# Query and key projections of a Flamingo block: evacuated 128 partitions wide into staging tiles, with DMAs placing the halves

## The chip, the core and the metric

The kernel runs on one core of one Trainium2 chip. Its time is the device time of one execution, in microseconds, as the median of repeated runs. TensorE (PE), VectorE (DVE), ScalarE (ACT) and GpSimd (POOL) each run their own instruction list, and SyncE (SP) issues all the DMAs. The engines meet only at semaphores.

## What is computed

A gated cross-attention layer, then a gated mixture of experts, for 8 batches of 512 tokens with 256 channels. The context has 512 rows of 128 channels; there are 16 heads of 64.

```
h = layernorm(x)
q, k, v = h @ Wq, ctx @ Wk, ctx @ Wv            # 16 heads of 64
out = softmax(q k^T / 8) v @ Wo + bo
x = x + tanh(g_xattn) * out
h2 = layernorm(x);  top-2 of 8 experts by softmax(h2 @ gate_w^T)
x = x + tanh(g_ffn) * sum_e comb_e * (h2 @ W_e^T + b_e)
```

## The kernel before

**Precision.** Most products are made from split operands: a value is rounded to fp32r ("hi") and the rest is kept as a second fp32r tile ("lo"). A projection is then three matmuls for each pair of tiles (hi·hi, hi·lo, lo·hi). ACT makes the hi part from PSUM, then DVE subtracts it from PSUM to get the lo part.

**Batches and slots.** Every engine walks the same order: batch, head h of 16, tile t of 4 (128 queries). One (h, t) is a slot. The first batch (FIRST), six in a hardware loop of two rounds of three (LOOP) and the last (LAST) have the same slots; EPI finishes the experts of the last batch. In each slot TensorE does two things for attention: the scores of tile (h, t), transposed, as two matmuls into a bank of ST (`scores`, L1044 and L1047), and one plain score matmul into a bank of MX for a tile six slots ahead (`maximum`, L1037). DVE reduces the MX bank to a row maximum (L767), SyncE carries the 128 maxima by a DMA into one row of QB (`row`, L432), and L1047 adds them to the scores, so that exp needs no further shift. ACT takes the exp (L596) and copies it to fp16 (L621), POOL makes its lo part (L514), and `values` (L1057) multiplies by V once per head. MX and ST have two banks each.

**Jobs.** Everything else is a list of jobs written out by hand in `PLACED`, which says in which slot TensorE makes it: `q`, `k`, `v` projections, `ot` (turned outputs), `wo`, the router and the experts of the batch before. Jobs share three PSUM banks; `job_ready` counts those made by PE, `job_hi` those that ACT has taken, `job_free` those whose bank is free again. A pair of heads p has a job ("q", p) and a job ("k", p), each a bank of 128 partitions (head 2p in partitions 0 to 63, head 2p+1 in 64 to 127) by 512 tokens. Pairs 2 to 7 are made in the batch itself, pairs 0 and 1 of the next batch in heads 12 to 15. q is made at (0,2), (2,3), (4,2), (6,1), (8,1), (10,1), (12,1), (14,1), and k at (1,1), (3,0), (5,0), (7,0), (8,3), (10,3), (12,3), (14,3); a job is taken by ACT and DVE one slot later (`taken_in`).

**The tiles of the scores.** For each head, QA holds the hi part of q in both halves of the partitions, KA the hi part of k above its lo part, KB the hi part of k, and QB the lo part of q, with the row of maxima in partition 64 (and ones there in KB). So L1044 gives hi·hi + lo·hi and L1047 gives hi·lo and the shift. All four tiles have six places, that is three pairs of heads.

**Evacuation of q and k.** The two heads of a job lie in different halves of the bank, so each is moved by its own instruction of 64 partitions: ACT writes QA[0:64] or KA[0:64] twice (L552, L553), DVE writes QB[0:64] (L739) or KA[64:128] (L744) twice. One DMA of 256 KB then copies QA[0:64] to QA[64:128], or KA[0:64] to KB[0:64], for both heads (`copy`, L427). TensorE waits for these copies at the first slot of a pair (`k_dup`) and, for a pair ahead, at (h even, 2) (`q_dup`).

**SyncE's order.** In `step`, for each slot: the row of the maximum, then the copy of a q or k job whose hi part is taken in that slot. Between batches it stores `acc` (L477) and loads `kvin` (L450). At head 5 it loads the next x (L467). In FIRST it also loads Wo and the expert weights (L457).

Of the kernel before, what the change touches and what calls it, by code (L numbers as in the profile page):

```python
# [177 lines left out]
class Iteration:  # L178
# [9 lines left out]
    def pair_slot(self, name):  # L188

        ahead = PAIRS if self.kind != PRO and name in NEXT_JOBS else 0  # L190
        return self.head_slot(2 * (name[1] + ahead))

    def start(self, lists):
# [46 lines left out]
def build(nc, x, kv_t, g_xattn, g_ffn, wq, wk, wv, wo, bo, gate_t, expert_t, expert_b, out):  # L240
# [5 lines left out]
    with ctx:  # L246
# [96 lines left out]
        job_ready, job_hi, job_free = sem("job_ready"), sem("job_hi"), sem("job_free")  # L343
        q_dup = [sem("q_dup0"), sem("q_dup1")]
        k_dup = [sem("k_dup0"), sem("k_dup1")]
        max_ready, max_free = sem("max_ready"), sem("max_free")
# [22 lines left out]

        def dup_count(b, p):  # L370
            return 16 * (b * (PAIRS // 2) + (p // 2 + 1))

# [33 lines left out]
        def _(sp):  # L406
# [11 lines left out]

            def copy(it, name):

                kind, p = name
                s = it.pair_slot(name)
                heads = slice(s, s + 2)
                dst, src, copied = ((QA[HEAD:P, heads, :], QA[0:HEAD, heads, :], q_dup) if kind == "q" else
                                    (KB[0:HEAD, heads, :], KA[0:HEAD, heads, :], k_dup))
                sp.wait_ge(job_hi, it.done(HI, name))
                sp.dma_start(dst.bitcast(F32), src.bitcast(F32)).then_inc(copied[p % 2], 16)  # L427

            def row(it, h, t):

                sp.wait_ge(max_free, tile_count(it.b, h, t) + 2)
                sp.dma_start(QB[HEAD:HEAD + 1, it.head_slot(h), t * P:(t + 1) * P].bitcast(F32),  # L432
                             nmax[:, h % 2, t:t + 1].bitcast(F32), allow_slow_non_contiguous=True)\
                  .then_inc(row_in[h % 2], 16)

            pro = Iteration(PRO, 0, 0)
            for name in [name for name in JOBS[PRO] if name[0] in "qk"]:
                if name == ("q", 1):
                    for t in range(TT):
                        row(pro, 0, t)  # L440
                copy(pro, name)
            for t in range(TT // 2):
# [10 lines left out]
            def step(it, h):  # L453
# [84 lines left out]
        def _(act):  # L538
# [6 lines left out]
            def take_hi(it, name):  # L545
# [3 lines left out]
                kind = name[0]  # L549
                if kind in ("q", "k"):  # L550
                    dst, s = (QA if kind == "q" else KA), it.pair_slot(name)
# [90 lines left out]
        def _(dve):  # L642
# [44 lines left out]
            def take(it, name):  # L687
# [47 lines left out]
                dve.wait_ge(job_hi, it.done(HI, name))  # L735
                if kind == "q":
                    s = it.pair_slot(name)
# [189 lines left out]
        def _(pe):  # L927
# [112 lines left out]
            def scores(it, h, t):  # L1040

                b, s = it.b, it.head_slot(h)
                pe.wait_ge(st_free, tile_count(b, h, t))
                pe.matmul(st_bank(h, t)[:, :], KA[:, s, tile(t)], QA[:, s, :], start=True, stop=False)  # L1044
                if t == 0:
                    pe.wait_ge(row_in[h % 2], row_count(b, h))
                pe.matmul(st_bank(h, t)[:, :], KB[0:HEAD + 1, s, tile(t)], QB[0:HEAD + 1, s, :],  # L1047
                          start=False, stop=True).then_inc(st_ready, 1)
# [16 lines left out]
            for name in JOBS[PRO]:  # L1065
# [6 lines left out]
                if name == ("q", 1):  # L1072
                    pe.wait_ge(job_free, pro.done(JOBS, ("k", 0)) + BANKS)
                    pe.wait_ge(q_dup[0], dup_count(0, 0))
                    for t in range(TT):
# [6 lines left out]
            def slot(it, h, t):  # L1082
                b, kind = it.b, it.kind
                p, ahead = h // 2, (h + 2) // 2 % PAIRS
                if h % 2 == 0 and t == 0:
                    pe.wait_ge(k_dup[p % 2], dup_count(b, p))
                for part in PE_ORDER[h % 2][t].split():
                    if part == "scores":
                        scores(it, h, t)
                    elif part == "maximum":  # L1090
                        if maximum_at(kind, h, t):
                            if h % 2 == 0 and t == TT // 2:
                                pe.wait_ge(job_free, (it.done_before if ahead == 1 else it.done)(JOBS, ("k", ahead))
                                           + BANKS)
                                pe.wait_ge(q_dup[ahead % 2], dup_count(b if ahead else b + 1, ahead))
                            maximum(it, *maximum_at(kind, h, t))
# [41 lines left out]
```

## Time and profile before

| | |
|---|---|
| runs | 1210.83, 1213.07, 1218.82 us |
| median | 1213.07 us |
| profiled execution | 1210.17 us, of which the span of instructions is 1208.5 us |
| granted TensorE clock | 0.989 |
| busy: PE, DVE, ACT, POOL | 94%, 81%, 70%, 54% |
| mean DMA queue load (q1) | 20.3% of 16 engines |

The span runs from the first to the last instruction. A matmul is pipelined and its end is modelled, so a PE that is 94% busy may still lose time between matmuls; what it waited for stands in the chain of waits and in the idle times ahead of a group. The first batch lies at about 9 to 154 us, the six looped ones from 154 to 1018 us, the last up to 1145 us, and the rest is the epilogue.

### The profile page before, as it was taken

The numbers are of one execution on the slowest core, as the hardware profiler recorded it, in microseconds if no ns is written. First come the engines' busy times: TensorE is split into PE (matmuls) and PEld (weight loads), VectorE is DVE, ScalarE is ACT, GpSimd is POOL, SyncE is SP. The second block draws the span as 40 slices with busy tenths as digits, with TensorE's granted clock in tenths as the row PEclk, the third lists the DMA queues.
The fourth block names the chain that finished last, engine by engine and source line by source line (L and its number), as shares of the span: only waits on it lengthen the run. The fifth ranks groups of instructions, "written<-read, shape, count | busy, mean of one in ns | idle before, by whom it ended". The sixth has DMA issues, their size and how long they took to land.

```text
span 1208.5 us, 30873 instructions
## 1 busy us (share of the span) xinstructions
PE 1135.7 (94%) x10592; PEld 913.4 (76%) x10592; DVE 979.0 (81%) x1945; ACT 849.6 (70%) x1531; POOL 648.0 (54%) x579
## 2 busy tenths in 40 slices
PE   4888999999999999999899999999999999999968
PEld 3677777788778887788777887778877788778846
DVE  7788878987898778987789877898778887897646
ACT  4888888676876678676786768867687677866610
POOL 2566666455655547455564545645556455654610
PEclk8999999999999999999999999999999999999979
DMA  4333212122221122221222112211122121121000
GB/s 133 78 85 79 37 37 54 29 37 45 37 53 29 28 54 36 46 37 27 57 37 45 28 37 45 54 36 28 41 50 45 28 37 40 33 37 36 2 19 17
DMA packets 97521, 51.79 MB, mean 43 GB/s; under 512 B 77000, under 2 KB 86608, under 8 KB 97360
## 3 DMA queue, kind: packets, MB, share of 16 engines
q1 hardware_dynamic: 97360, 49.74, 20.3%
q8 instruction: 89, 1.46, 0.5%
q14 instruction: 72, 0.59, 0.2%
HBM read 11.68 MB, written 4.19 MB: 13 GB/s over the span
## 4 chain that ended last, share of the span: by engine, by line
PE 70%; DVE 15%; issue 7%; DMA 3%; ACT 3%; SPq 1%; DVEq 0%; POOL 0%; ACTq 0%
PE MB L934 30%; PE PV L1057 12%; PE MX L1037 8%; PE ST L1047 7%; PE ST L1044 7%; DVE nmax L767 3%; DVE KA L744 3%; PE MB L944 3%; DMA QB<-nmax 2%; DVE QB L739 1%; PE MB L1014 1%; DVE stats L656 1%; DVE w L879 1%; SPq L432 1%; DVE m L886 1%
## 5 line engine op out<-in xcount | busy, mean ns | idle before, releaser
L514 POOL TENSOR_TENSOR p_s<-pf,p_s 128x512 f16<-128x512 f32 x512 | 594.7, 1169 | 496.1 <-ACT p_s L621 492.5
L596 ACT ACTIVATE pf<-ST 128x512 f32<-128x512 f32 x512 | 306.2, 599 | 193.0 <-PE ST L1047 186.3
L767 DVE TENSOR_REDUCE nmax<-MX 128x1 fp32r<-128x512 f32 x512 | 347.2, 685 | 69.0 <-PE MX L1037 60.9
L621 ACT ACTIVATE p_s<-pf 128x512 f16<-128x512 f32 x512 | 318.1, 629 | 45.1 <-PE PV L1057 42.0
L1037 PE MATMUL MX<-KA,QA 128*128 128x512 f32 x512 | 216.9, 426 | 18.6 <-DVE nmax L767 15.2
L1057 PEld LDWEIGHTS PV<-v_s,p_s 128*128 128x128 f16 x6144 | 193.6, 98 | 33.6 <-issue 24.7
L1047 PE MATMUL ST<-QB,KB 65*128 65x512 f32 x512 | 204.8, 400 | 7.2 <-DMA QB<-nmax 7.0
L1057 PE MATMUL PV<-v_s,p_s 128*128 128x65 f16 x6144 | 209.0, 194 | 1.3 <-POOL p_s L514 1.3
L1044 PE MATMUL ST<-QA,KA 128*128 128x512 f32 x512 | 206.2, 403 | 3.6 <-ACT pf L596 3.1
L934 PE MATMUL MB<-ex_s,x2t_s 128*128 128x512 f32 x708 | 188.8, 402 | 3.2 <-DVE KA L744 3.2
L934 PEld LDWEIGHTS MB<-ex_s,x2t_s 128*128 128x128 f32 x708 | 128.1, 188 | 34.9 <-DVE KA L744 6.3
L1037 PEld LDWEIGHTS MX<-KA,QA 128*128 128x128 f32 x512 | 97.1, 190 | 54.3 <-DVE nmax L767 32.6
L722 DVE SCALAR_TENSOR_TENSOR acc<-MB,comb,acc 128x256 f32<-128x256 f32 x236 | 113.8, 482 | 23.6 <-PE MB L934 16.5
L1047 PEld LDWEIGHTS ST<-QB,KB 65*128 65x128 f32 x512 | 96.3, 188 | 31.8 <-DMA QB<-nmax 13.4
L1044 PEld LDWEIGHTS ST<-QA,KA 128*128 128x128 f32 x512 | 97.0, 189 | 23.0 <-issue 6.7
L934 PEld LDWEIGHTS MB<-wo_s,ot_s 128*128 128x128 f32 x768 | 100.0, 188 | 7.2 <-DVE ot_s L754 1.7
L934 PE MATMUL MB<-xt_s,wq_s 128*128 128x512 f32 x384 | 102.3, 402 | 1.7 <-issue 1.5
L934 PE MATMUL MB<-wo_s,ot_s 128*128 128x256 f32 x768 | 101.5, 282 | 1.4 <-DVE ot_s L754 1.4
L739 DVE TENSOR_TENSOR QB<-MB,QA 64x512 fp32r<-64x512 f32 x128 | 87.6, 684 | 17.7 <-ACT QA L553 16.8
L744 DVE TENSOR_TENSOR KA<-MB,KA 64x512 fp32r<-64x512 f32 x128 | 88.3, 690 | 14.0 <-ACT KA L553 10.2
L934 PEld LDWEIGHTS MB<-xt_s,wq_s 128*128 128x128 f32 x384 | 73.9, 193 | 19.9 <-issue 1.8
L754 DVE TENSOR_TENSOR ot_s<-MB,ot_s 128x512 fp32r<-128x512 f32 x64 | 44.2, 690 | 46.0 <-ACT ot_s L559 45.4
(120 smaller groups left out, 1113.4 us busy)
## 6 DMA issues: line engine op xcount, KB each, us to landing
QA<-QA SPq DMA_DIRECT2D x64, 256.0 KB, 3.0
KB<-KA SPq DMA_DIRECT2D x64, 256.0 KB, 3.0
QB<-nmax SPq DMA_DIRECT2D x512, 0.5 KB, 1.9
xin<-x SPq DMA_DIRECT2D x8, 512.0 KB, 4.0
out<-acc SPq DMA_DIRECT2D x8, 512.0 KB, 3.2
kvin<-kv_t SPq DMA_DIRECT2D x8, 256.0 KB, 4.2
acc<-expert_t SPq DMA_DIRECT2D x8, 256.0 KB, 3.3
acc<-wo SPq DMA_DIRECT2D x4, 256.0 KB, 3.3
```

The source lines that it names most:

```text
L514: pool.tensor_tensor(p_s[:, h % 2, 1, t, :], pf[:, t, :], p_s[:, h % 2, 0, t, :], ALU.subtract)\
L596: act.activation(pf[:, t, :], st_bank(h, t)[:, :], ACT.Exp, bias=P_SHIFT, scale=SCALE)\
L621: act.activation(p_s[:, h % 2, 0, t, :], pf[:, t, :], ACT.Copy).then_inc(p_hi, 1)
L722: last = dve.scalar_tensor_tensor(acc[:, t, :], m[:, DIM * i:DIM * (i + 1)], comb[:, t, 2 * e + i:2 * e + i + 1], acc[:, t, :], ALU.mult, ...
L739: last = dve.tensor_tensor(QB[0:HEAD, s + i, :], m[HEAD * i:HEAD * i + HEAD, :], QA[0:HEAD, s + i, :].bitcast(F32), ALU.subtract)
L744: last = dve.tensor_tensor(KA[HEAD:P, s + i, :], m[HEAD * i:HEAD * i + HEAD, :], KA[0:HEAD, s + i, :].bitcast(F32), ALU.subtract)
L767: dve.tensor_reduce(nmax[:, h % 2, t:t + 1], MX[t % 2][:, :], AX.X, ALU.max, negate=True)\
L934: last = pe.matmul(dst, s, m, start=(k == 0), stop=(k == n - 1))
L1037: pe.matmul(MX[t % 2][:, :], QA[:, s, tile(t)], KA[:, s, :], start=True, stop=True)\
L1044: pe.matmul(st_bank(h, t)[:, :], KA[:, s, tile(t)], QA[:, s, :], start=True, stop=False)
L1047: pe.matmul(st_bank(h, t)[:, :], KB[0:HEAD + 1, s, tile(t)], QB[0:HEAD + 1, s, :], start=False, stop=True).then_inc(st_ready, 1)
L1057: last = pe.matmul(PV[:, t * (HEAD + 1):(t + 1) * (HEAD + 1)], p_s[:, h % 2, i, k, tile(t)], v_s[:, j, k, h % HEADS, :], start=(k == 0 and ...
```

## The change

In LOOP, FIRST and LAST (not in the prologue, PRO), ACT moves a q or k job with one instruction of 128 partitions into a staging tile, `q_hl[:, 0]` or `k_hl[:, 0]`, and DVE writes the rest into `[:, 1]` with one instruction. DMAs of 128 KB then place the halves, two for each placement. `copy_first`, one slot later than `copy` stood, issues four: for q both halves of QA; for k both KA[0:64] and then, after a wait for `job_free`, both KA[64:128]. `copy_second(it, h)`, at the first slot of an even head, issues four for the next pair: KB[0:64] and QB[0:64] in turn, because KB and QB now have four places (two pairs) in place of six, and the pair that held them must be through. Each pair so takes 12 DMAs of 128 KB where it took two of 256 KB. New waits: ACT, before it fills a staging tile, waits for the copies of the pair before out of it (and for DVE to have used it); DVE waits likewise before a lo part; TensorE waits at (h even, 0) for KB and QB and at (h even, 2) for QA and KA of the following pair.

```diff
@@ tiles @@
-        QB = sb("QB", [P, 2 * SLOTS, TOKENS], F32R)
+        QB = sb("QB", [P, 4, TOKENS], F32R)
-        KB = sb("KB", [P, 2 * SLOTS, TOKENS], F32R)
+        KB = sb("KB", [P, 4, TOKENS], F32R)
+        q_hl = sb("q_hl", [P, 2, TOKENS], F32R)
+        k_hl = sb("k_hl", [P, 2, TOKENS], F32R)
@@ sync @@
+            def copy_first(it, name):
+                kind, p = name
                 s = it.pair_slot(name)
                 sp.wait_ge(job_hi, it.done(HI, name))
+                for i in range(2):
+                    rows = slice(HEAD * i, HEAD * (i + 1))
+                    if kind == "q":
+                        sp.dma_start(QA[0:HEAD, s + i, :].bitcast(F32), q_hl[rows, 0, :].bitcast(F32))\
+                          .then_inc(qa_in[p % 2], 16)
+                        sp.dma_start(QA[HEAD:P, s + i, :].bitcast(F32), q_hl[rows, 0, :].bitcast(F32))\
+                          .then_inc(qa_in[p % 2], 16)
+                    else:
+                        sp.dma_start(KA[0:HEAD, s + i, :].bitcast(F32), k_hl[rows, 0, :].bitcast(F32))\
+                          .then_inc(ka_in[p % 2], 16)
+                if kind == "k":
+                    sp.wait_ge(job_free, it.done(JOBS, name) + BANKS)
+                    for i in range(2):
+                        rows = slice(HEAD * i, HEAD * (i + 1))
+                        sp.dma_start(KA[HEAD:P, s + i, :].bitcast(F32), k_hl[rows, 1, :].bitcast(F32))\
+                          .then_inc(ka_in[p % 2], 16)
+
+            def copy_second(it, h):
+                p = h // 2 + 1
+                if h == 0:
+                    sp.wait_ge(job_free, it.start(JOBS) + BANKS)
+                else:
+                    sp.wait_ge(job_free, it.done(JOBS, ("k", p % PAIRS)) + BANKS)
+                for i in range(2):
+                    rows = slice(HEAD * i, HEAD * (i + 1))
+                    sp.dma_start(KB[0:HEAD, 2 * (p % 2) + i, :].bitcast(F32), k_hl[rows, 0, :].bitcast(F32))\
+                      .then_inc(kb_in[p % 2], 16)
+                    sp.dma_start(QB[0:HEAD, 2 * (p % 2) + i, :].bitcast(F32), q_hl[rows, 1, :].bitcast(F32))\
+                      .then_inc(qb_in[p % 2], 16)
...
                     if maximum_at(it.kind, h, t):
                         row(it, *maximum_at(it.kind, h, t))
-                    for name in taken_in(it.kind, h, t):
-                        if name[0] in "qk":
-                            copy(it, name)
+                    if h % 2 == 0 and t == 0 and not (it.kind == FIRST and h == 0) and \
+                            not (it.kind == LAST and h == HEADS - 2):
+                        copy_second(it, h)
+                    if (h, t) != (0, 0):
+                        for name in taken_in(it.kind, *((h, t - 1) if t else (h - 1, TT - 1))):
+                            if name[0] in "qk":
+                                copy_first(it, name)
@@ scalar, take_hi @@
+                if kind in ("q", "k") and it.kind != PRO:
+                    p = name[1]
...
+                    before = p - 1 if p >= 2 else p - 1 + PAIRS
+                    if not early_pair(it, before):
+                        if kind == "q":
+                            act.wait_ge(qa_in[before % 2], qa_count(it, before))
+                        else:
+                            act.wait_ge(ka_in[before % 2], ka_count(it, before))
+                            act.wait_ge(kb_in[before % 2], kb_count(it, before))
+                    last = act.activation((q_hl if kind == "q" else k_hl)[:, 0, :], m[:, :], ACT.Copy)
@@ vector, take @@
+                if kind in ("q", "k") and it.kind != PRO:
...
+                    if not early_pair(it, before):
+                        if kind == "q":
+                            dve.wait_ge(qb_in[before % 2], qb_count(it, before))
+                        else:
+                            dve.wait_ge(ka_in[before % 2], ka_count(it, before))
+                    last = dve.tensor_tensor(hl[:, 1, :], m[:, :], hl[:, 0, :].bitcast(F32), ALU.subtract)
@@ tensor @@
                 if h % 2 == 0 and t == 0:
-                    pe.wait_ge(k_dup[p % 2], dup_count(b, p))
+                    pe.wait_ge(kb_in[p % 2], kb_count(it, p))
+                    if not early_pair(it, p):
+                        pe.wait_ge(qb_in[p % 2], qb_count(it, p))
...
                             if h % 2 == 0 and t == TT // 2:
...
+                                    pe.wait_ge(ka_in[following % 2], ka_count(it, following))
+                                pe.wait_ge(qa_in[following % 2], qa_count(it, following))
```

## Rows read from the trace of the kernel before

**Rows 1.** The profile page: chain of waits by engine and by line.
```profile
PE 70%; DVE 15%; issue 7%; DMA 3%; ACT 3%; SPq 1%; DVEq 0%; POOL 0%; ACTq 0%
PE MB L934 30%; PE PV L1057 12%; PE MX L1037 8%; PE ST L1047 7%; PE ST L1044 7%; DVE nmax L767 3%; DVE KA L744 3%; PE MB L944 3%; DMA QB<-nmax 2%; DVE QB L739 1%; PE MB L1014 1%; DVE stats L656 1%; DVE w L879 1%; SPq L432 1%; DVE m L886 1%
```

**Rows 2.** Table by stretch, one looped batch.
```profile
core 0: us, PE busy (x) PEld busy (x) DVE busy (x) ACT busy (x) POOL busy (x), PEclk, DMA share, GB/s
...
296.60:440.30 143.70, 139.78 (x1326) 113.16 (x1325) 119.82 (x240) 105.56 (x191) 80.08 (x71) 1.00 0.20 40
```

**Rows 3.** Chain of waits of 370 to 441 us, by line.
```profile
by line: PE MB L934 44.3%; PE PV L1057 14.5%; PE MX L1037 9.7%; PE ST L1044 9.7%; PE ST L1047 9.6%; PE MB L944 3.7%; issue 2.1%; PE MB L1014 1.8%; DVE nmax L767 1.0%; ACT ot_s L559 0.8%; DVE acc L722 0.8%; SPq L477 0.7%; SPq L432 0.7%; PE M
```

**Rows 4.** Groups by shape: busy us, mean ns, idle before and its releaser.
```profile
L739 DVE TENSOR_TENSOR QB<-MB,QA 64x512 fp32r<-64x512 f32 x128 | 87.6, 684 | 17.7 <-ACT QA L553 16.8
...
L754 DVE TENSOR_TENSOR ot_s<-MB,ot_s 128x512 fp32r<-128x512 f32 x64 | 44.2, 690 | 46.0 <-ACT ot_s L559 45.4
...
L553 ACT ACTIVATE QA<-MB 64x512 fp32r<-64x512 f32 x64 | 38.1, 596 | 0.7
...
L559 ACT ACTIVATE ot_s<-MB 128x512 fp32r<-128x512 f32 x64 | 38.1, 595 | 5.0 <-PE MB L944 5.0
```

**Rows 5.** DMA issues: size, median us to landing.
```profile
QA<-QA SPq DMA_DIRECT2D x64, 256.0 KB, 3.0
...
QB<-nmax SPq DMA_DIRECT2D x512, 0.5 KB, 1.9
```

**Rows 6.** Timeline of SyncE: a copy and the rows behind it.
```profile
480.98 0.54 SPq L427 DMA_DIRECT2D QA<-QA  x1
```

**Rows 7.** Landing of the row issued at 481.6, by its line.
```profile
L432 SPq DMA_DIRECT2D QB<-nmax x1: 533/533/533, 481.6 to 481.6; - x1
...
DMA to landing us min/median/max: 3.1/3.1/3.1
```

**Rows 8.** Chain of waits of 440 to 446.5 us: start, us, what.
```profile
441.70 0.78 SPq L432
...
442.60 3.45 DMA QB<-nmax
...
446.09 0.50 PE ST L1047
```

**Rows 9.** Timeline, third batch, heads 0 to 2: start, us, idle in brackets.
```profile
301.73 1.39 DVE L739 TENSOR_TENSOR QB<-MB,QA 64x512 fp32r<-64x512 f32 x2 [1.14 <-ACT QA L553]
...
308.17 1.39 DVE L744 TENSOR_TENSOR KA<-MB,KA 64x512 fp32r<-64x512 f32 x2 [1.06 <-ACT KA L553]
...
311.60 4.95 SPq L432 DMA_DIRECT2D QB<-nmax  x4
...
314.82 0.40 PE L1037 MATMUL MX<-KA,QA 128*128 128x512 f32 x1
```

**Rows 10.** Timeline, heads 2 to 4 of the same batch.
```profile
320.09 1.38 DVE L739 TENSOR_TENSOR QB<-MB,QA 64x512 fp32r<-64x512 f32 x2
...
324.83 1.39 DVE L744 TENSOR_TENSOR KA<-MB,KA 64x512 fp32r<-64x512 f32 x2
...
327.63 4.73 SPq L432 DMA_DIRECT2D QB<-nmax  x4
...
331.61 0.40 PE L1037 MATMUL MX<-KA,QA 128*128 128x512 f32 x1
```

**Rows 11.** Timeline, heads 6 and 7, DVE.
```profile
352.17 1.38 DVE L739 TENSOR_TENSOR QB<-MB,QA 64x512 fp32r<-64x512 f32 x2
...
359.78 1.39 DVE L744 TENSOR_TENSOR KA<-MB,KA 64x512 fp32r<-64x512 f32 x2
```

**Rows 12.** Chain of waits of 100 to 125 us, first batch.
```profile
102.86 0.69 DVE KA L744
...
105.82 1.88 DMA QB<-nmax
...
107.75 0.50 PE ST L1047
```

More of the change, by code:

```diff
@@ L191, in pair_slot, with copied @@
         return self.head_slot(2 * (name[1] + ahead))
+    def copied(self, p):
+        return 4 * self.b + p // 2
     def start(self, lists):
@@ L368, in head_count, with qa_count, ka_count, qb_count @@
             return b * HEADS + (h + 1)
-        def dup_count(b, p):
-            return 16 * (b * (PAIRS // 2) + (p // 2 + 1))
+        def qa_count(it, p):
+            return 64 * it.copied(p) + 16
+        def ka_count(it, p):
+            return 64 * it.copied(p)
+        def qb_count(it, p):
+            return 32 * it.copied(p)
+        def kb_count(it, p):
+            return 32 * it.copied(p) + 16
+        def early_pair(it, p):
+            return it.kind == FIRST and p < 2
         late = [(wo[256 * k:256 * (k + 1), :].rearrange("(c p) n -> p c n", p=P),
@@ L417, in _, with copy_early @@
             sp.dma_start(gt_f[:, :, :], gate_t.rearrange("(c p) e -> p c e", p=P)).then_inc(small_in, 16)
-            def copy(it, name):
+            def copy_early(it, name):
+                kind, p = name
+                heads = slice(2 * p, 2 * p + 2)
+                dst, src, copied = ((QA[HEAD:P, heads, :], QA[0:HEAD, heads, :], qa_in) if kind == "q" else
+                                    (KB[0:HEAD, heads, :], KA[0:HEAD, heads, :], kb_in))
+                sp.wait_ge(job_hi, it.done(HI, name))
+                sp.dma_start(dst.bitcast(F32), src.bitcast(F32)).then_inc(copied[p % 2], 16)
@@ L440, in _ @@
                         row(pro, 0, t)
-                copy(pro, name)
+                copy_early(pro, name)
             for t in range(TT // 2):
@@ L735, in take @@
                 dve.wait_ge(job_hi, it.done(HI, name))
-                if kind == "q":
+                if kind in ("q", "k") and it.kind != PRO:
+                    p = name[1]
+                    before = p - 1 if p >= 2 else p - 1 + PAIRS
+                    hl = q_hl if kind == "q" else k_hl
+                    if not early_pair(it, before):
[4 more added lines that the diff above has]
+                    last = dve.tensor_tensor(hl[:, 1, :], m[:, :], hl[:, 0, :].bitcast(F32), ALU.subtract)
+                elif kind == "q":
                     s = it.pair_slot(name)
@@ L1046, in scores @@
                     pe.wait_ge(row_in[h % 2], row_count(b, h))
-                pe.matmul(st_bank(h, t)[:, :], KB[0:HEAD + 1, s, tile(t)], QB[0:HEAD + 1, s, :],
+                pe.matmul(st_bank(h, t)[:, :], KB[0:HEAD + 1, h % 4, tile(t)], QB[0:HEAD + 1, h % 4, :],
                           start=False, stop=True).then_inc(st_ready, 1)
@@ L1073, in _ @@
                     pe.wait_ge(job_free, pro.done(JOBS, ("k", 0)) + BANKS)
-                    pe.wait_ge(q_dup[0], dup_count(0, 0))
+                    pe.wait_ge(qa_in[0], 16)
                     for t in range(TT):
@@ L1092, in slot @@
                             if h % 2 == 0 and t == TT // 2:
-                                pe.wait_ge(job_free, (it.done_before if ahead == 1 else it.done)(JOBS, ("k", ahead))
-                                           + BANKS)
-                                pe.wait_ge(q_dup[ahead % 2], dup_count(b if ahead else b + 1, ahead))
+                                following = h // 2 + 1
+                                if early_pair(it, following):
+                                    pe.wait_ge(job_free, it.start(JOBS) + BANKS)
+                                else:
+                                    pe.wait_ge(ka_in[following % 2], ka_count(it, following))
+                                pe.wait_ge(qa_in[following % 2], qa_count(it, following))
                             maximum(it, *maximum_at(kind, h, t))
```

20 lines of the change are left out of this document (11 added, 9 removed).

## Prediction

> **What bounds the kernel now.** I read the chain of waits first, because an average share of busy time hides which wait ends last. It is 70% TensorE and 15% DVE; the second halves of the k evacuations (L744) are 3% of it and those of q (L739) 1% [rows 1]. So TensorE sets the pace in most places, and DVE in some. The table by stretch says the same of one looped batch: of 143.7 us TensorE is busy 139.8, DVE 119.8 and ACT 105.6 [rows 2]. Then I read the chain batch by batch. From head 8 on (370 to 441 us) it is TensorE nearly throughout, and no evacuation of q or k is among its entries [rows 3]: whatever the change saves or delays there by less than the slack of DVE and ACT is worth nothing. The stretches where an evacuation does end the wait are four: the row of maxima that TensorE awaits at the start of head 1 [rows 8], k of pair 2 in head 1 [rows 9], q and k of pair 3 [rows 10], q and k of pair 5 with the routing around them [rows 11]. The rest of the argument is about these four, seven times over, and about the first batch.
>
> **What the wide instructions save.** One DVE instruction of 64 partitions takes 684 ns, one of 128 partitions 690 ns; for ACT it is 596 and 595 ns [rows 4]. The width costs nothing, so each q or k job loses a whole instruction: 0.7 us of DVE and 0.6 us of ACT. For 124 such jobs outside the prologue that is 85 us of DVE and 74 us of ACT, but it counts only in the stretches above. k of pair 2: DVE stood idle 1.06 us until ACT had made the second half [rows 9], so both savings lie in line, 1.3 us. Pair 3: two of DVE's instructions go, in a stretch where DVE works without a break, 1.4 us. Pair 5: again 1.4 us. Together 4.1 us a batch, if nothing else becomes late.
>
> **What the DMAs cost.** A copy of 256 KB lands 3.0 us after its issue, a row of 0.5 KB 1.9 us [rows 5]; a copy of 128 KB lies between, and halfway, 2.45 us, is my value, with both ends kept. Issuing one costs SyncE 0.54 us, and the next begins 0.64 after it [rows 6, 7]: four take 2.4 us. Half of the 1.1 us of transfer is about 0.55 us, a little under the pace of issue, so within a burst nothing should pile up much. The Trainium skill (DMA: Bandwidth & Descriptors, "Rules for kernel authors") says that two transfers to disjoint partition halves aren't worth splitting, because both use the same 16 engines and serialize. That speaks against the two halves of each placement. The same page's fit (its cost of one DMA, 2.0 us and the bytes at 436 GB/s) gives an estimate of 2.3 us for 128 KB, by which each sum below would come out 0.15 us lower. The trace shows the sharing: a row issued right behind a copy landed after 3.1 us and not 1.9 [rows 7].
>
> **Where k now arrives by DMA.** Before, DVE wrote the lo part of k into KA in place. Now SyncE issues it after the row of slot (h, t) two slots behind the job. Call M the end of DVE's maximum there. The row takes 0.5 us, then come four issues, the last beginning at M + 2.3 and landing at M + 4.8 (4.2 to 5.3 with the ends above). TensorE wants it at its `maximum` of slot (h even, 2), and `scores`, `values` or jobs are queued behind that.
> - Pair 2: SyncE's row issue at 311.60 marks M, and TensorE's maximum is at 314.82, 3.2 us later [rows 9]. With M 1.3 us earlier, KA is there at old M + 3.5. So the stage gains nothing and loses 0.3 us (gain of 0.3 to loss of 0.8).
> - Pair 3: 327.63 and 331.61 [rows 10], 4.0 us. M is 1.4 us earlier, KA at old M + 3.4: a gain of 0.6 us instead of 1.4 (0.1 to 1.2).
> - Pair 5 has the same four slots, but with two expert jobs in them, so TensorE comes later; pairs 6, 7, 0 and 1 have a slot more, 2.2 us (143.7 / 64). I take these as in time. The gain of 1.4 us stays.
>
> **The rows behind `copy_second`.** In slot (h even, 0) four issues now stand between the row of that slot and the next. A slot takes 2.2 us on average, so SyncE is mostly free again in time, and the row of head h + 1, tile 3, is wanted only three slots later. The exception is h = 0. SyncE comes there late from storing `acc` and loading `kvin`; its first row is issued at 441.70 to 442.48, the decisive one at 442.60, it lands 3.45 us later and TensorE starts at once [rows 8]. Four issues in between move the second to 445.0. The backlog of the store will be through by then, so I take 2.6 us to landing (between the 1.9 of a free queue and 3.45 as now), 447.6 in place of 446.05: a loss of 1.6 us (0.9 to 2.4). Here the DMA is on the path that sets the end in every batch from the second on. DVE waits at the same time: the lo part of q of pair 2 may begin only when QB of pair 1 has been copied out, about 442.5 + 2.4 + 2.4 = 447.3. Its like in the batch before began at 301.73, after 1.14 us of idle time [rows 9], one batch of 143.7 us earlier than 445.4. This 1.9 us lies beside TensorE's stall and I cost it at nothing; without that cover it would be another 1 us.
>
> **The same wait elsewhere.** For the other q jobs the lo part comes two slots after `copy_second`, some 4 us, against 0.5 + 1.8 + 2.45 = 4.75 after M. DVE will stand idle up to 0.7 us and has one instruction of 0.7 us less to do: even. In heads 8 to 15 DVE's slack covers it.
>
> **Sum of a looped batch.** +0.3 - 0.6 - 1.4 + 1.6 = -0.1 us; seven batches about -1 us. With all ends good it is -0.3 - 1.2 - 1.4 + 0.9 = -2.0 a batch, -14 in all; with all bad, and half of pair 5's gain lost, +0.8 - 0.1 - 0.7 + 2.4 = +2.4, +17 in all.
>
> **First batch.** It has no expert jobs, so slots are shorter, and TensorE is often released by a row: an evacuation of k ends at 103.55, the row takes 1.88 us from 105.82, and the matmul begins at 107.75 [rows 12]. My estimates, from that one row and the prices above: six heads in which a burst stands before such a row, at 1.0 us each (0.6 of issue and 0.7 of landing, less some slack), 6 us; with KA of pairs 2 and 3, where less time is left than in a looped batch, 4 us; and with about 12 evacuations on the chain that lose an instruction, 0.7 us each, 8 us. Net +2 us (-6 to +10). In the last batch head 13 is released by its row in the same way: +1 us. The prologue keeps its own evacuations.
>
> **Total.** -1 + 2 + 1 = +2 us on the profiled 1210.2 us. The median of the runs is 2.9 us above that execution, so 1215 us. Within 1% is what a measurement of this kernel can't tell from no change: 1201 to 1225.
>
> **Rivals.**
> - *Bursts that pile up (slower).* If the copies of a burst hold up one another, so that the last lands 3.5 us or more after its issue, every burst becomes a wait: KA of pairs 2 and 3 comes 1 us later than reckoned, the row of head 1 lands after 3.45 us, and the rows of heads 2 and 5, just behind a burst of q or of `copy_second`, come late too. At 1 us for each of these that is some 4 us a batch above my sum, 28, and in the first batch 8: 1250 us, 1240 if only part of it shows. It decides from a landing of M + 5.5. For it: rows behind one copy already land 1.2 us late [rows 7], and traffic per pair goes from 0.5 to 1.5 MB. Against it: 0.55 us of transfer at an issue every 0.6. 0.18.
> - *DVE waits for QB (slower).* If the lo part of q waits over 1 us in each pair, and DVE's queue with its maxima behind it, the second halves of the batches lose too: 5 pairs by 0.5 us by 7, 17 us: 1232 us. Against it: DVE is 83% busy there and waits for TensorE between. 0.09.
> - *The savings go through (faster).* If a copy of 128 KB lands in little over 1.9 us and SyncE's delay at head 0 is hidden by the backlog that now holds up the row, the good ends apply: -14 - 6 - 0 gives 1193 us. For it: the chain names these evacuations [rows 1]. 0.13. That the wide instructions save nothing is excluded by rows 4.
> - *My forecast*, 1203 to 1225: 0.60.
>
> **Range and chances.** 1200 to 1236 leaves out the far part of the first and third rival, 2 in 10. Faster by over 1%: 0.13. Slower by over 1%: the two slower rivals less their near edge, 0.25. Within: 0.62.
>
> **What the profile after should show.** Evacuations of q and k as 62 instructions each of 128x512 on ACT and DVE, beside the prologue's of 64; DVE busy about 85 us less, ACT about 73 less. TensorE waiting for KA by DMA at slots (2,2) and (4,2); the row of head 1 landing 1 to 2.5 us later in each looped batch; SyncE issuing twice as much. The DMA share well up from 20%, as 1.5 MB go in place of 0.5 for each pair. Looped batches of 143 to 145 us. I am wrong if bursts land later than 5.5 us after M, if rows in the second halves of batches become late, or if TensorE's wait at head 1 turns out shorter than now.

## The result, and the profile after

The changed kernel takes 1291.9 us (median of 4 runs, 1287.8 to 1295.2) against 1214.3 us for the kernel before in the same runs: a ratio of 1.064, with an interval of 1.060 to 1.068. It is 6.4% slower. I had forecast 1215 us and no change, so the sign and the size were both wrong.

The page of the profiled execution of the changed kernel (1287.8 us), with the groups and the DMA issues that answer to those of before [rows 1, 4, 5]:

```profile
span 1286.0 us, 31656 instructions
...
PE 1159.3 (90%) x10592; PEld 931.0 (72%) x10592; DVE 880.8 (68%) x1821; ACT 774.1 (60%) x1407; POOL 647.0 (50%) x579
...
PE 61%; SPq 10%; DVE 10%; DMA 9%; issue 6%; ACT 3%; POOL 0%; DVEq 0%; ACTq 0%
PE MB L1018 26%; PE PV L1141 10%; PE MX L1121 7%; PE ST L1131 6%; PE ST L1128 6%; DMA QB<-nmax 4%; DVE nmax L851 3%; DMA KA<-k_hl 3%; PE MB L1028 3%; DMA QB<-q_hl 3%; SPq L488 2%; SPq L480 2%; SPq L482 2%; SPq L462 1%; ACT ot_s L633 1%
...
L819 DVE TENSOR_TENSOR q_hl<-MB,q_hl 128x512 fp32r<-128x512 f32 x62 | 42.7, 689 | 71.7 <-DMA QB<-q_hl 64.7
L623 ACT ACTIVATE q_hl<-MB 128x512 fp32r<-128x512 f32 x62 | 37.0, 597 | 65.3 <-PE MB L1018 65.3
...
QA<-q_hl SPq DMA_DIRECT2D x248, 128.0 KB, 2.4
```

DVE is busy 880.8 us in place of 979.0 and ACT 774.1 in place of 849.6, more than the 85 and 74 us reckoned. That part works as described: 62 wide instructions each of q and k, at 689 and 597 ns. But the chain of waits now holds 10% of SyncE's queue, where it held 1%, and 9% of DMA, where it held 3% [rows 1]. TensorE's share of the chain falls from 70 to 61%. The waits of the changed kernel, in total, times and longest, and as the last row the same wait in the kernel before:

```profile
DVE q_hl L819 <- DMA QB<-q_hl: 64.7, 31, 6.4
PEld ST L1131 <- DMA QB<-nmax: 61.2, 43, 6.4
PE ST L1131 <- DMA QB<-nmax: 43.4, 31, 6.0
...
PE MX L1121 <- DMA KA<-k_hl: 31.2, 19, 2.3
...
PE ST L1047 <- DMA QB<-nmax: 7.0, 10, 2.0
```

A matmul and its weight load can both wait for the same thing, so the second and third rows aren't to be added. Before, TensorE's matmuls waited 7.0 us for rows of maxima; now 43.4. The wait for KA is new, 31.2 us; all but 0.8 us of it lies in heads 2 and 4, and in the seven batches behind the first it comes to 3.9 us a batch. DVE's wait for the copy out of the staging tile is new too, 64.7 us in 31 of 62 jobs, and the longest is 6.4 us.

The waits for rows lie in three places, by the timeline of TensorE. In the first batch they are 15.8 us, where they were 3.3. At the first slot of head 1, behind the `copy_second` of head 0, they are 15.6 us in seven batches, where they were 3.4. The rest lies mostly at heads 2 and 7 of the looped batches. Two rows of head 1:

```profile
327.74 0.79 PE L1131 MATMUL ST<-QB,KB 65*128 65x512 f32 x1 [2.32 <-DMA QB<-nmax]
...
637.77 0.80 PE L1131 MATMUL ST<-QB,KB 65*128 65x512 f32 x1 [6.00 <-DMA QB<-nmax]
```

The second is the longest of all and stands alone. It is where the hardware loop begins its second round: SyncE's queue has 4.0 us of `issue` there, between the store and the load, and `copy_second` behind that. In the kernel before the same place had the longest wait too, 2.0 us.

**Where SyncE loses its time.** The timeline of SyncE's queue in the third batch, heads 1 to 2 and then 3 to 4; an entry is start, length and what was issued:

```profile
338.43 1.18 SPq L462 DMA_DIRECT2D KA<-k_hl  x2
339.71 1.18 SPq L468 DMA_DIRECT2D KA<-k_hl  x2
341.00 0.54 SPq L488 DMA_DIRECT2D QB<-nmax  x1
341.59 0.59 SPq L480 DMA_DIRECT2D KB<-k_hl  x1
...
343.51 0.60 SPq L482 DMA_DIRECT2D QB<-q_hl  x1
344.21 8.70 SPq L488 DMA_DIRECT2D QB<-nmax  x5
353.02 0.54 SPq L457 DMA_DIRECT2D QA<-q_hl  x1
...
354.89 0.60 SPq L459 DMA_DIRECT2D QA<-q_hl  x1
355.59 1.70 SPq L488 DMA_DIRECT2D QB<-nmax  x1
357.41 1.17 SPq L462 DMA_DIRECT2D KA<-k_hl  x2
```

The four issues of k (L462, L468), a row (L488) and the four of `copy_second` (L480, L482) follow each other without a gap from 338.4 to 344.1 us; the row at 344.21 is the last that TensorE needs at the start of head 3. In this trace it costs little there: the weight load waits 0.3 us for it and the matmul nothing, as TensorE has just lost 2.1 us on KA (below). Later the burst of q of pair 3 (353.0 to 355.5) and one row stand in front of that of k of pair 3. I had priced each burst by itself.

The chain there, as start, length and what:

```profile
337.15 0.69 DVE nmax L851
...
340.30 2.33 DMA KA<-k_hl
342.85 0.49 PE MX L1121
```

The maximum ends at 337.84, KA has landed at 342.63 and TensorE begins at 342.85: 4.8 us to the landing, as reckoned, and 5.0 to the matmul. The landing (2.3 us) is near what I had taken. But TensorE ran out of other work and stood idle 2.1 us before this matmul, as its timeline shows in brackets:

```profile
342.85 0.49 PE L1121 MATMUL MX<-KA,QA 128*128 128x512 f32 x1 [2.12 <-DMA KA<-k_hl]
```

**What comes behind some of the waits.** The table by stretch (TensorE's busy time, weight loads, DVE, ACT, POOL, granted clock, DMA share):

```profile
core 0: us, PE busy (x) PEld busy (x) DVE busy (x) ACT busy (x) POOL busy (x), PEclk, DMA share, GB/s
...
328.00:331.00 3.00, 3.00 (x44) 2.48 (x45) 2.17 (x4) 0.60 (x1) 0.00 (x0) 0.51 0.05 6
343.00:346.00 3.00, 3.00 (x20) 2.70 (x20) 1.66 (x3) 0.50 (x2) 0.11 (x1) 1.00 0.72 167
362.00:365.00 3.00, 3.00 (x8) 2.32 (x9) 1.89 (x3) 0.00 (x0) 1.93 (x2) 0.50 0.75 173
...
386.00:389.00 3.00, 3.00 (x56) 2.62 (x55) 2.55 (x10) 1.54 (x3) 0.46 (x1) 1.00 0.05 6
...
48.00:51.00 3.00, 3.00 (x46) 2.48 (x46) 0.75 (x2) 1.11 (x2) 1.97 (x2) 0.50 0.27 50
```

and, from the chain of waits, six matmuls of a job with their moving tile of 512 columns, first in head 2 (at the full clock), then right behind the wait of head 4:

```profile
345.46 1.40 PE MB L1018 x6
...
362.53 2.56 PE MB L1018 x6
```

The stretches at 328 and 362 us follow waits of 2.3 and 2.0 us and show a granted clock of 0.51 and 0.50, that is the lower of TensorE's two levels, 1.2 GHz. The work is slower there: six such matmuls take 2.56 us in place of 1.40. But the length of the wait alone doesn't decide it. The stretch at 343 us follows the wait of 2.1 us for KA and shows 1.00, as the one behind a wait of 1.5 us does (386), and in the first batch a wait of 1.0 us, with two of 0.5 and 0.3 us just ahead of it, is followed by 0.50 (48).

How much of the loss that is can be bounded. The mean clock over the whole span is 0.967; it was 0.989. As full-speed time, 0.033 of 1286.0 us is missing, 42 us, against 0.011 of 1208.5, 13 us. TensorE wasn't busy in all of that time, so up to 29 of the 77.5 us are paid in clock and not in waiting. The busy time says nearly the same: TensorE is busy 1159.3 us in place of 1135.7, 23.6 more for the same work, and the other 54 us are idle time. The Trainium skill tells of this (TensorE: Matmul & The Clock Gate, "HAM oscillation — how this bites in real kernels"): where TensorE waits for a DMA between groups of matmuls its clock drops, and the next group begins at the lower rate. The trace agrees behind two of the three waits of 2.0 us and more in the third batch, by the 0.51 and 0.50 above, and not behind the other; the forecast had no term for it.

**Which batches lose.** The same table for the second and third batch:

```profile
169.20:317.40 148.20, 141.22 (x1324) 113.92 (x1325) 105.60 (x222) 95.29 (x175) 79.96 (x70) 0.99 0.43 93
317.40:470.20 152.80, 142.54 (x1326) 115.46 (x1325) 106.71 (x224) 95.50 (x175) 79.87 (x70) 0.98 0.42 94
```

They take 148.2 and 152.8 us where one took 143.7 [rows 2], with TensorE's busy time at 141.2 and 142.5 for 139.8: of the 9.1 us of the third, 2.8 lie in slower work and 6.3 in waiting. The first batch loses more: it ends at 169.2 us, where it ended at about 154, and 12.5 us of that are waits for rows (15.8 for 3.3).

### The profile page after: what moved, and what is told of

Same layout as the page of the kernel before. It is cut to its first block, busy times and chain, and to the rows that moved or that the text cites. A ratio compares the mean times of both kernels' runs of the same rounds, so it can differ in the third digit from the quotient of the medians.

```text
span 1286.0 us, 31656 instructions
## 1 busy us (share of the span) xinstructions
PE 1159.3 (90%) x10592; PEld 931.0 (72%) x10592; DVE 880.8 (68%) x1821; ACT 774.1 (60%) x1407; POOL 647.0 (50%) x579
## 4 chain that ended last, share of the span: by engine, by line
PE 61%; SPq 10%; DVE 10%; DMA 9%; issue 6%; ACT 3%; POOL 0%; DVEq 0%; ACTq 0%
PE MB L1018 26%; PE PV L1141 10%; PE MX L1121 7%; PE ST L1131 6%; PE ST L1128 6%; DMA QB<-nmax 4%; DVE nmax L851 3%; DMA KA<-k_hl 3%; PE MB L1028 3%; DMA QB<-q_hl 3%; SPq L488 2%; SPq L480 2%; SPq L482 2%; SPq L462 1%; ACT ot_s L633 1%
## 5 line engine op out<-in xcount | busy, mean ns | idle before, releaser
L1121 PE MATMUL MX<-KA,QA 128*128 128x512 f32 x512 | 219.7, 431 | 47.8 <-DMA KA<-k_hl 31.2
L1131 PE MATMUL ST<-QB,KB 65*128 65x512 f32 x512 | 209.8, 410 | 43.8 <-DMA QB<-nmax 43.4
L1141 PEld LDWEIGHTS PV<-v_s,p_s 128*128 128x128 f16 x6144 | 200.6, 99 | 37.0 <-issue 30.4
L1141 PE MATMUL PV<-v_s,p_s 128*128 128x65 f16 x6144 | 216.2, 196 | 1.3 <-POOL p_s L574 1.3
L1018 PE MATMUL MB<-xt_s,wq_s 128*128 128x512 f32 x384 | 108.3, 420 | 1.5 <-issue 1.5
L1018 PEld LDWEIGHTS MB<-xt_s,wq_s 128*128 128x128 f32 x384 | 77.9, 203 | 20.3 <-issue 1.8
L819 DVE TENSOR_TENSOR q_hl<-MB,q_hl 128x512 fp32r<-128x512 f32 x62 | 42.7, 689 | 71.7 <-DMA QB<-q_hl 64.7
L623 ACT ACTIVATE q_hl<-MB 128x512 fp32r<-128x512 f32 x62 | 37.0, 597 | 65.3 <-PE MB L1018 65.3
```

The lines of the kernel that those rows point to most:

```text
L819: last = dve.tensor_tensor(hl[:, 1, :], m[:, :], hl[:, 0, :].bitcast(F32), ALU.subtract)
L1018: last = pe.matmul(dst, s, m, start=(k == 0), stop=(k == n - 1))
L1121: pe.matmul(MX[t % 2][:, :], QA[:, s, tile(t)], KA[:, s, :], start=True, stop=True)\
L1131: pe.matmul(st_bank(h, t)[:, :], KB[0:HEAD + 1, h % 4, tile(t)], QB[0:HEAD + 1, h % 4, :], start=False, stop=True).then_inc(st_ready, 1)
L1141: last = pe.matmul(PV[:, t * (HEAD + 1):(t + 1) * (HEAD + 1)], p_s[:, h % 2, i, k, tile(t)], v_s[:, j, k, h % HEADS, :], start=(k == 0 and ...
```

## The experiments

Times are medians; each ratio is to the kernel before on the same chip, in the same job.

**Only one of the two staged.** Which half costs? In the first, k is evacuated in place as before and KB has six places again; q is staged.

```diff
-                if kind in ("q", "k") and it.kind != PRO:
+                if kind == "q" and it.kind != PRO:          # ACT and DVE; k falls to the old branch
...
+            def copy_k(it, name):                            # SyncE, where copy stood
+                s = it.pair_slot(name)
+                sp.wait_ge(job_hi, it.done(HI, name))
+                sp.dma_start(KB[0:HEAD, s:s + 2, :].bitcast(F32), KA[0:HEAD, s:s + 2, :].bitcast(F32))\
+                  .then_inc(kb_in[name[1] % 2], 16)
```

> Only q is staged; k is evacuated as before, into KA and KB by itself, and its 256 KB copy stands where it stood. Per pair SyncE then issues 7 copies in place of 12. SyncE theory (issues in front of rows and behind each other make rows and KA late): TensorE's idle time on KA copies, 31 us, is gone, and copy_second is two issues, so rows of odd heads are late by about 1.5 us and not 3 to 4: 1225 to 1240 us. Bytes theory (1.5 MB a pair load the DMA engines): 1.0 MB a pair leaves half the loss, 1250 us. Staging theory (DVE waits for QB copies before its lo part): that wait is all on q's side, so the loss mostly stays, 1265 us.

The second is its mirror image: q in place, k staged.

> Only k is staged; q is evacuated as before, into QA and QB, with its 256 KB copy where it stood. 7 copies a pair. SyncE theory: the waits for KA at the third slot of heads 2 and 4 stay nearly whole, with the slow-clock stretches behind them, and rows are less late: 1240 to 1255 us. Bytes theory: 1250 us, as with the other half. Staging theory: the wait for QB is gone, 1225 us.

Measured: 1230.3 us with q staged (1.014, 1.012 to 1.017), 1244.8 us with k staged (1.027, 1.023 to 1.030). Both fit the SyncE theory's numbers; the staging theory's 1265 and 1225 have the wrong order, and the bytes theory, by which they are equal, misses the first by 20 us. The two losses are 17 and 31 us, 48 in sum, where the whole change loses 77.5: the halves hurt each other. With k staged TensorE still waits for KA:

```profile
PE MX L1123 <- DMA KA<-k_hl: 25.9, 17, 2.9
```

With q staged there is no such wait; the matmuls wait 17.5 us for rows.

**Issues without data.** The kernel before gets the same number of further DMAs at the same places, but nobody waits for them.

```diff
+            def spare_copies(it, what, h, t):     # 3 at the places of copy_first, 4 at those of copy_second
+                ...
+                if not (it.kind == FIRST and n < 2):
+                    sp.wait_ge(spare_in[side], 16 * count)          # two bursts back
+                at = (QB, KB)[side]
+                for i in range(mine[n][3]):
+                    ...                           # 8 KB: at[96:128, i, 0:64] <- wk_s[0:32, 0, 0:64]
+                    sp.dma_start(dst.bitcast(F32), src.bitcast(F32)).then_inc(spare_in[side], 16)
```

> The kernel before, and at the places of copy_first and copy_second three and four further DMAs of 8 KB each, from a weight tile into unused partitions of QB and KB, for which nobody waits but SyncE itself, two bursts later. So issues as in the change, hardly a byte more, no new wait on data. SyncE theory: rows behind copy_second come 2.5 to 4 us late, TensorE waits at odd heads: 1235 to 1255 us, about half of the loss. Bytes theory and staging theory: no change, 1214 us within 0.5%.

> The same with 128 KB in each further DMA, so the bytes of the change too. SyncE theory: as with 8 KB, 0 to 8 us more for rows that land behind a burst. Bytes theory: most of the loss, 1270 us. Staging theory: no change.

Measured: 1258.8 us with 8 KB each (1.036, 1.033 to 1.039) and 1301.9 us with 128 KB each (1.072, 1.069 to 1.075). So the issues with 8 KB each cost 45 us, more than half of the loss. This is the cleanest row of the study: no copy that anyone else waits for, hardly a byte more, a row lands after 2.0 us (median) in place of 1.9, SyncE never has to wait for a spare burst, and TensorE waits for rows as long as in the changed kernel. The total, and the timeline of TensorE at the starts of heads 3 and 5 of the third batch:

```profile
PE ST L1092 <- DMA QB<-nmax: 45.4, 34, 4.9
...
340.36 0.50 PE L1092 MATMUL ST<-QB,KB 65*128 65x512 f32 x1 [0.77 <-DMA QB<-nmax]
...
358.86 0.50 PE L1092 MATMUL ST<-QB,KB 65*128 65x512 f32 x1 [1.23 <-DMA QB<-nmax]
```

Of the 45.4 us, 21.7 lie at heads 3 and 5, where bursts meet, and 12.3 at head 1. In the changed kernel heads 3 and 5 have only 3.3 of 43.4. There TensorE has lost its time a few slots earlier on KA; that this is why the rows no longer show is my reading, and no run separates the two.

The 128 KB version costs 43 us more, and there the SyncE theory, which allowed 8, fails: bytes count as well. (Its copies go to 32 partitions in pieces of 4 KB or to 16 in pieces of 8 KB, and it keeps the 0.5 MB of the old copies, so it is no exact likeness.)

**The changed kernel with few bytes.** The other way round: all issues and waits of the change, an eighth of the bytes. Outside the first batch only 64 of 512 columns are moved, so the scores there come from stale columns.

```diff
+            def cols(it):
+                return slice(0, TOKENS if it.kind == FIRST else 64)
...
-                        sp.dma_start(KA[0:HEAD, s + i, :].bitcast(F32), k_hl[rows, 0, :].bitcast(F32))\
+                        sp.dma_start(KA[0:HEAD, s + i, cols(it)].bitcast(F32), k_hl[rows, 0, cols(it)].bitcast(F32))\
```

> The changed kernel, with its 12 copies a pair, their order and all waits, but outside the first batch each copy moves 64 columns of 512 only (16 KB in place of 128 KB), so scores of those batches are computed from stale columns. If the spare issues of 8 KB (1259 us) and of 128 KB (1302 us) split the loss rightly, bytes are worth about half of it: 1245 to 1260 us. If the loss is all SyncE's issue order and the waits for staged data, the time stays at 1280 to 1290 us.

Measured: 1262.7 us (1.042, 1.038 to 1.046). Bytes are worth 29 us of the 77.5; 48 remain with issues, and waits for landings that are now 1.8 us in place of 2.4. That lies 3 us outside my upper figure.

**Which burst.** The spare issues of 8 KB once only at the places of `copy_second`, once only at those of `copy_first`.

```diff
 # only copy_second's places: the call for q and k jobs is left out
-                        for name in taken_in(...):
-                            if name[0] in "qk":
-                                spare_copies(it, name, h, t)
```

> The kernel before with only the four spare issues of 8 KB at the place of copy_second, none at the place of copy_first. The prediction held that SyncE is mostly free again in time for the next row, except at head 0: that gives 5 to 12 us, 1219 to 1226. If this place alone carries the 45 us of all spare issues: 1250.

```diff
 # only copy_first's places: the call at the first slot of an even head is left out
-                    if h % 2 == 0 and t == 0 and ...:
-                        spare_copies(it, "second", h, t)
```

> The kernel before with only the three spare issues of 8 KB at each place of copy_first. If one burst at a time is harmless and only two in a row delay a row: 1216 to 1222 us, and with the 5 to 12 us of the other half less than 45 in sum. If the number of issues counts wherever they stand: 1240, as 6 of 10.

Measured: 1233.0 us (1.015, 1.014 to 1.017) and 1224.6 us (1.008, 1.006 to 1.010): 18 and 10 us, 28 in sum, and 45 together. The first is above the 5 to 12 us that the forecast's step allowed, the second a little above the 2 to 7 that I expected. The 17 us that neither has are the price of bursts that meet: at heads 3 and 5 TensorE waits 2.0 us for rows in the first run and 1.3 in the second, and 21.7 with both. A row behind one burst mostly finds slack, but not at head 1: there the first run has 11.8 of its 18.3 us of waits for rows, 1.4 to 1.6 us in five of the last six batches and 3.9 at the start of the loop's second round.

**Another order.** The changed kernel with the same 12 copies of 128 KB, in smaller bursts for q and for `copy_second`, and k's copies earlier.

```diff
+                    for name in taken_before(1):
+                        if name[0] == "k":
+                            copy_first(it, name, (), lo=True)        # KA[64:128], ahead of the row
                     if maximum_at(it.kind, h, t):
                         row(it, *maximum_at(it.kind, h, t))
+                    if h % 2 == 0 and t < 2 and ...:
+                        copy_second(it, h, "qk"[t])                  # QB at (h, 0), KB at (h, 1)
+                    for n in (1, 2):
+                        for name in taken_before(n):
+                            if name[0] == "q":
+                                copy_first(it, name, (n - 1,))       # one half a slot
+                    for name in taken_in(it.kind, h, t):
+                        if name[0] == "k":
+                            copy_first(it, name, (0, 1))             # KA[0:64], one slot earlier
```

> The changed kernel with the same 12 copies of 128 KB, but never more than two between two rows: the hi part of k one slot earlier, its lo part ahead of the row, q's halves one slot apart, QB at (h even, 0) and KB at (h even, 1). Same issues, same bytes. If bursts are the cause (SyncE's or the engines'), rows are late by 1.3 us at most and KA lands 1.3 us earlier: 1235 to 1255 us. If the total of issues or bytes is the cause, no gain: 1285 to 1295 us.

Measured: 1252.9 us (1.031, 1.028 to 1.034). With every issue, byte and staging tile of the change in it, the order alone gives back 39 of the 77.5 us. But the edit doesn't do what the text before it says. k's hi part goes out behind one row and its lo part ahead of the next, so four copies stand between two rows, and six where half of a q job falls there too, as in SyncE's timeline of the third batch:

```profile
345.92 0.54 SPq L458 DMA_DIRECT2D QA<-q_hl  x1
...
347.20 1.18 SPq L463 DMA_DIRECT2D KA<-k_hl  x2
348.49 2.45 SPq L469 DMA_DIRECT2D KA<-k_hl  x2
351.04 0.54 SPq L491 DMA_DIRECT2D QB<-nmax  x1
```

The trace has 46 such runs of six. TensorE waits 26.3 us for rows in place of 43.4, but up to 4.6 us for one behind six copies (119.72 us), and 20.3 us for KA and QA in place of 31.2 for KA. So the run shows that the order counts, with issues and bytes as they were. It doesn't show that short bursts alone would do it, since k's hi part also goes out one slot earlier. DVE's wait for QB falls with it, from 64.7 us to:

```profile
DVE q_hl L831 <- DMA QB<-q_hl: 16.6, 8, 4.4
...
PE MX L1133 <- DMA QA<-q_hl: 13.2, 6, 2.5
```

The second row is what the order of my making adds: the second half of q of pair 3 now comes behind k's and is awaited in head 4.

**copy_second behind the row.** One slot later, so that the row of the odd head goes out first.

```diff
-                    if h % 2 == 0 and t == 0 and not (it.kind == FIRST and h == 0) and \
+                    if h % 2 == 0 and t == 1 and not (it.kind == FIRST and h == 0) and \
```

> The changed kernel with copy_second one slot later, behind the row that head h + 1 waits for. Rows of odd heads are then issued at once; QB is copied out 2.2 us later, and DVE's lo part of q, behind it the maxima, wait for that. If the rows are the larger cost: 1265 to 1280 us. If the staged tile is: 1290 to 1310.

Measured: 1304.6 us, 13 us slower than the change itself (1.077, 1.072 to 1.081), within the range that I had for the staged tile. TensorE waits less for the rows and DVE waits twice as long:

```profile
DVE q_hl L819 <- DMA QB<-q_hl: 133.4, 44, 9.0
...
PE ST L1131 <- DMA QB<-nmax: 34.7, 23, 2.9
```

TensorE's own wait for DVE's lo part of q rises from 4.5 to 20.5 us. So the single staging tile sets a due time for `copy_second` on one side and the row one on the other. Neither end of that slot is free.

**ACT issues copy_second.** The same four lines with `act` in place of `sp`, at the end of ACT's slot.

```diff
@@ sync @@
-                    if h % 2 == 0 and t == 0 and not (it.kind == FIRST and h == 0) and ...:
-                        copy_second(it, h)
@@ scalar, end of the slot @@
+                if h % 2 == 0 and t == 0 and not (it.kind == FIRST and h == 0) and ...:
+                    copy_second(it, h)           # act.wait_ge(job_free, ...), then four act.dma_start
```

> The changed kernel with the four issues of copy_second moved from SyncE to ACT's queue, at the end of the same slot. ACT has 40% idle time. If the row of the next slot is late because SyncE issues four copies ahead of it, that lateness (3 to 4 us at odd heads) goes, and with it the waits of 104 us for QB<-nmax: 1245 to 1260 us. If the bytes in the DMA engines hold the row, it stays at 1280 to 1295 us.

Measured: 1309.0 us (1.077, 1.074 to 1.080), slower still, against my 1245 to 1260. (The 104 us in that text add the waits of matmuls and of their weight loads, which aren't to be added.) Two things I had not counted. ACT's own work stands behind its issues:

```profile
321.78 0.47 ACTq L685 DMA_DIRECT2D KB<-k_hl  x1
...
322.93 0.87 ACTq L685 DMA_DIRECT2D KB<-k_hl  x1
...
324.79 0.63 ACT L695 ACTIVATE p_s<-pf 128x512 f16<-128x512 f32 x1 [2.79 <-issue]
```

ACT is idle for 2.8 us there, and 40% idle time on average was no cover, because exp and its copy release TensorE's next bank and POOL. And the wait for KA grows from 31.2 to 63.8 us, though SyncE has less to do; the wait for rows falls to 27.6. The chain of waits shows where: the last copy of k for pair 2, issued at 341.14 us and in the changed kernel at 340.30, lands after 4.65 us in place of 2.33.

```profile
PE MX L1121 <- DMA KA<-k_hl: 63.8, 26, 4.8
...
PE ST L1131 <- DMA QB<-nmax: 27.6, 27, 3.7
...
341.14 4.65 DMA KA<-k_hl
```

ACT's four copies are issued from 338.07 to 340.85 and SyncE's four of k from 339.23 to 341.93, so two queues issue copies of 128 KB at once. That they hold one another up fits the copies issued from ACT too, which land after 2.9 and 3.4 us (medians); from SyncE's queue they took 2.3 and 2.4.

**Improving the kernel before.** If SyncE's order ahead of a row is worth that much, the row of head 1 [rows 8] should gain from an emptier queue. First only the load of the next context goes behind the row of slot (0, 1); then also the store of `acc`, in four of seven batches.

```diff
+                    if (h, t) == (0, 1):
+                        if it.kind == LOOP and it.turn != 1:
+                            store(Iteration(LOOP, it.b - 1, it.turn - 1))
+                        load_context(it)
```

> The kernel before, with the load of the next context (kvin) issued behind the row of slot (0, 1) and not ahead of the batch's first row. If rows at head 1 are late because SyncE and the DMA engines are busy with the store and this load, the row lands 1 us earlier in seven batches: 1207 us, 0.3 to 0.7% faster. Otherwise no change.

> The kernel before with the context's load behind the row of slot (0, 1), as in the run where it was 0.2% faster, and in four of the seven batches the store of acc too. The row of head 1 then has nothing ahead of it there: 0.3 to 0.6% faster than before, 1208 to 1211 us. If the row is not on the path any more, as with the load alone: 0.2%.

Measured: 1212.6 us (0.998, 0.996 to 1.000), which misses the 1207 of the first text, and 1208.3 us (0.996, 0.994 to 0.997), within the second's. The second is 0.4% faster than the kernel before, and so faster than both kernels. TensorE's waits for rows fall only from 7.0 to 5.6 and 5.4 us; where the rest of the 6.5 us comes from isn't shown. The second's timeline of SyncE at the start of the fourth batch has five rows ahead of the store (L481), and the load of the context (L450) behind it:

```profile
434.32 7.99 SPq L432 DMA_DIRECT2D QB<-nmax  x5
442.58 0.40 SPq L481 DMA_DIRECT2D out<-acc  x1
443.31 0.36 SPq L450 DMA_DIRECT2D kvin<-kv_t  x1
```

## Why the prediction was wrong, step by step

- *What bounds the kernel*: right as to the place for the looped batches: in the third, TensorE's long stalls lie in heads 1 to 4, where I had looked for them, and one of 1.5 us at head 7, where I had not. The first batch was not understood well enough.
- *What the wide instructions save*: the prices were right (689 and 597 ns), the 4.1 us a batch were not realised. For k of pair 2 I reckoned that the maximum M comes 1.3 us earlier. In the chain after, what precedes it is TensorE's own work and `ot_s` (DVE's maximum begins at 337.15 behind it), not the evacuation.
- *What the DMAs cost*: right. 128 KB lands in 2.4 us, and the last copy of k 4.8 us after M. (By my own pace of 0.64 us the last issue begins at M + 2.4, not 2.3; measured 2.46.) "Nothing should pile up much" holds for the landings, but not for the bytes: the few-bytes run puts 29 us on them. The Trainium skill's rule against splitting by partition halves (DMA: Bandwidth & Descriptors, "Rules for kernel authors") pointed the right way. The same page's fit (its cost of one DMA, given for DMAs issued from GpSimd) makes 2.3 us for 128 KB as an estimate, as good as my halfway value: the trace has 2.3 and 2.4.
- *Where k arrives by DMA*: the first step that failed. I set the loss at 0.3 us for pair 2 and counted a gain of 0.6 for pair 3, a net gain of 0.3 a batch. TensorE stands idle 2.1 and 2.0 us there in the third batch, and 3.9 us a batch on average, 27.6 in seven. The places were right, the sizes were not. For pair 2 the saving before M, by which I had made 1.6 us into 0.3, did not come. For pair 3 I took M + 0.5 as the start of k's burst. The burst of q of the same pair is issued in the slot before, and k's begins at 357.41.
- *The rows behind `copy_second`*: the second step that failed, and not where I had looked. At head 1, the exception that I named, I had a loss of 1.6 us a batch. Measured are 12.2 us more of waits in seven batches, 1.7 a batch: right, though 4.0 of them fall into one batch. What failed is "A slot takes 2.2 us on average, so SyncE is mostly free again in time". It is true of one burst of 2.4 us, and false where `copy_first` of k in slot (1,3) or (3,2) stands next to it: nine issues in a row take 5.8 us (338.4 to 344.2). The spare issues show the price of that: 18 us for `copy_second` alone, 10 for the others, 45 together. I also had no term for rows of even heads behind a burst of q, nor for head 7, where the load of the next x stands ahead of `copy_second`.
- *The same wait elsewhere* (DVE's lo part of q): I called it even. It is 64.7 us of DVE's time in sum, because QB is copied out late wherever SyncE is late. TensorE's matmuls wait only 4.5 us for that lo part in the changed kernel. So the rival by which DVE waits for QB had its wait, and a small part in the loss. With `copy_second` behind the row it is no longer small (20.5 us).
- *First batch*: I had +2 us, and the second batch begins some 15 us later than before. The terms had the saved instructions (8 us) nearly cancel the bursts (10 us), at 1.0 us for each of six rows. Ten rows are awaited, at 1.6 us on average and 2.7 at most, 15.8 us in all.
- *The rivals*: the slower rival had bursts of copies that land 3.5 us after their issue. They land in 2.4; what piles up is SyncE's issue time. It was the nearest, and had 0.18. Its price, 1240 to 1250 us, falls short of 1292 by 42 to 52 us, of which the clock is up to 29.
- *Missing*: the clock, a term that I put at nothing without a reason; it is up to 29 of the 77.5 us. The kernel before gave no sign of it: its clock is 1.00 over 154 to 1018 us, even behind its one stall of 2.0 us there (592.51). I priced each wait at its own length.

## What to carry to other kernels

Count a DMA queue's issues as work of an engine: lay all of them out in order between the transfers that someone waits for, bursts of neighbouring jobs included, before asking how fast one lands. A queue that waits for over a quarter of the time on average (SyncE waits 345.5 of 1286.0 us for DVE's maxima alone) can be full for nine issues in a row at the one place where a small, urgent transfer stands behind them. Where TensorE is the bound, waits can cost more than their own length through its clock: here up to 29 us beside 54 us of added idle time.

## What the runs showed that I had not expected

TensorE's granted clock fell to 0.50 behind waits of 2.0 and 2.3 us and stayed at 1.00 behind one of 2.1 us in the same batch. A DMA issue took 0.5 to 0.9 us of ACT's queue, where SyncE's mostly takes 0.5 to 0.6, and the engine's instructions wait behind it. With the two queues issuing at once a copy of 128 KB landed after 4.65 us in place of 2.3. DMAs of 8 KB for which no engine waits made the kernel 3.6% slower, with rows landing as before (2.0 us for 1.9).
